# Decoder kernel on one core: softplus to PSUM, its product with u on VectorE, the step copied by ScalarE, and the convolution split around the last sum over states

## What is computed

```python
u, z = jnp.split(layer_norm(x) @ in_w, 2, axis=-1)            # 256 channels each
up = jnp.pad(u, ((0, 0), (3, 0), (0, 0)))
u = silu(cb + sum(up[:, k:k + L, :] * cw[:, k] for k in range(4)))
dbl = u @ xw
dt = softplus(dbl[..., :64] @ dtw + dtb)                      # the step
Bm, Cm = dbl[..., 64:80], dbl[..., 80:]
dA = exp(dt[..., None] * A)                                   # 16 states per channel
dBu = (dt * u)[..., None] * Bm[:, :, None, :]
h = dA_t * h + dBu_t                                          # over time
y = einsum('ben,bn->be', h, C_t)                              # sum over states
x = x + ((y + u * Dp) * silu(z)) @ ow
```

## Time and profile before

| | us |
|---|---|
| median of 3 runs | 1981.62 (1978.43 to 1983.26) |
| profiled execution | 1982.75 |
| its span | 1980.9 |

### The profile page before, as it was taken

The page is one execution under the profiler, slowest core; times in us unless marked ns, Lnnn a source line. Parts: engine busy times, 40 slices in busy tenths (PEclk is TensorE's granted clock), DMA queues, the critical chain, the costliest instruction groups (busy, mean ns, idle before and its releaser), DMA issues. The chain is left out here.

```text
span 1980.9 us, 23714 instructions
## 1 busy us (share of the span) xinstructions
PE 1417.6 (72%) x6931; PEld 753.8 (38%) x6931; DVE 1440.6 (73%) x2510; ACT 1137.4 (57%) x2515; POOL 1200.4 (61%) x759
## 2 busy tenths in 40 slices
PE   3899899995755556655566565556535899999968
PEld 2777577773311112211112121111101566666523
DVE  3666488885508988989898888999984566666734
ACT  2543688884636555555555555555533677777720
POOL 2000356560029999999999999999993243444400
PEclk8999899996567767777677776777866899999978
DMA  3000000000034323343322432333213000000000
GB/s 101 1 1 1 1 2 1 0 1 1 0 132 175 120 111 150 126 153 150 139 97 108 172 150 106 150 150 135 95 70 86 1 1 1 1 0 1 1 0 22
DMA packets 51970, 134.40 MB, mean 68 GB/s; under 512 B 19076, under 2 KB 28568, under 8 KB 39448
## 3 DMA queue, kind: packets, MB, share of 16 engines
q1 hardware_dynamic: 49112, 130.78, 17.4%
q10 hardware_dynamic: 2496, 2.36, 0.4%
q0 software_dynamic: 256, 0.01, 0.0%
HBM read 114.26 MB, written 18.87 MB: 67 GB/s over the span
## 5 line engine op out<-in xcount | busy, mean ns | idle before, releaser
L1470 POOL TENSOR_TENSOR ma_hs<-ma_dtuR,ma_Bt 128x1024 f32<-128x1024 f32 x256 | 596.4, 2353 | 7.1 <-DMA ma_dtuR<-ma_dtu_d 6.9
L1629 ACT ACTIVATE ps<-ma_dtR,ma_A 128x512 f32<-128x512 f32 x512 | 332.7, 682 | 361.2 <-DVE ma_hs L1763 221.3
L786 POOL TENSOR_TENSOR x_pr<-x_pr,x_rec 128x512 f32<-128x512 f32 x256 | 267.5, 1045 | 352.7 <-DVE x_rec L1035 352.7
L1547 PE MATMUL ps<-ma_hs,ma_fold 128*32 128x512 f32 x1024 | 198.4, 915 | 293.8 <-POOL ma_hs L1478 237.3
L1757 DVE TENSOR_TENSOR_SCAN ps<-ps,ma_hs 128x1024 f32<-128x1024 f32 x144 | 329.1, 2286 | 5.7 <-POOL ma_hs L1470 4.5
L1757 DVE TENSOR_TENSOR_SCAN ma_hs<-ps,ma_hs 128x1024 f32<-128x1024 f32 x112 | 255.9, 2284 | 47.1 <-POOL ma_hs L1470 38.6
L1001 ACT ACTIVATE x_pr<-x_sm,x_mx 128x256 f32<-128x256 f32 x512 | 254.5, 500 | 52.5 <-DVE x_mx L1026 52.0
L1478 POOL TENSOR_TENSOR ma_hs<-ma_hs,ma_Ct 128x1024 f32<-128x1024 f32 x112 | 262.9, 2348 | 0.4 <-DVE ma_hs L1757 0.4
L1547 PEld LDWEIGHTS ps<-ma_hs,ma_fold 128*32 128x32 f32 x1024 | 37.9, 144 | 422.4 <-issue 337.7
L1514 PE MATMUL ps<-ma_hn,ma_w_tap 128*128 128x512 f32 (+3 forms) x256 | 147.4, 741 | 59.7 <-ACT ma_hn L1647 47.8
L1763 DVE TENSOR_TENSOR ma_hs<-ps,ma_Ct 128x1024 f32<-128x1024 f32 x144 | 176.3, 1225 | 5.0
(11 more groups left out here) (308 smaller groups left out, 2466.8 us busy)
## 6 DMA issues: line engine op xcount, KB each, us to landing
ma_dtuR<-ma_dtu_d SPq DMA_DIRECT2D x32, 1024.0 KB, 7.0
ma_dtR<-ma_dt_d SPq DMA_DIRECT2D x32, 1024.0 KB, 8.9
ma_Bt<-ma_bc_d SPq DMA_DIRECT2D x16, 1024.0 KB, 5.0
ma_Ct<-ma_bc_d SPq DMA_DIRECT2D x16, 1024.0 KB, 6.9
ma_dtu_d<-ma_dtu SPq DMA_DIRECT2D x32, 256.0 KB, 2.0
ma_dt_d<-ma_dt SPq DMA_DIRECT2D x32, 256.0 KB, 2.3
ma_cwb<-in_L_attn_conv_w_dram SPq DMA_DIRECT2D x4, 512.0 KB
x_m<-in_mask_BxSxS_fk_dram SPq DMA_DIRECT2D x1, 2048.0 KB, 11.2
```

The source lines that it names most:

```text
L786: pool.tensor_tensor(pr[:, r, :, :], pr[:, r, :, :], rec[:, r, :].unsqueeze(2).broadcast_to([P, 2, L]), ALU.mult).then_inc(pr_done, 1)
L1470: pool.tensor_tensor(hs[:, k % SLOTS, :, :], dtuR[:, unit(f, h), q, :].unsqueeze(1).broadcast_to([P, 2, CH]), rows(Bt, k), ALU.mult).then_ ...
L1547: mm = pe.matmul(c.ps[q * E32:(q + 1) * E32, Y[h], :], fold[:, :], hs[:, (k0 + q) % SLOTS, a, :], start=False, stop=(j % 2 == 1 and a == 1 ...
L1629: e = act.activation(c.ps[:, 2 * (k % 2) + a, :], dtR[:, unit(f, h), q, :], ACT.Exp, scale=A[:, (f // QUARTERS) % 2, h, q, no:no + 1])
```

## The change

- VectorE writes softplus back to the PSUM banks PA and PB instead of `dt`, and then multiplies it with u into `dtu`. GpSimd's `dt_times_u` with its products and memsets is gone.
- ScalarE copies the step from PSUM to `dt`, all but the first position of each sequence (`copy_dt`, at t = 9). The large number is set once, at the start of the stage. SP waits for the product before it writes `dtu`, and for the copy before it writes `dt`. TensorE's next use of the banks waits for the copies.
- `NORM_D` is {1, 2, 3, 6, 8, 10, 12, 14, 15}: items 5, 7, 9, 11 and 13 go to GpSimd, and 6, 8, 10, 12 and 14 to VectorE. The two engines keep seven and nine items.
- The taps of channels 0 to 127 come before the last sum, those of 128 to 255 behind it.
- `inv_std`, `affine` (ScalarE) and `scaled_x` (VectorE) come one item earlier.

```diff
-    NORM_D = {1, 2, 3, 5, 7, 9, 11, 13, 15}
+    NORM_D = {1, 2, 3, 6, 8, 10, 12, 14, 15}
...
                         sp.dma_start(dtu_d[d, h], dtu[:, h, :]).then_inc(dt_out[h], 16)
+                        sp.wait_ge(dt_copied, 2 * F + h + 1)
                         sp.dma_start(dt_d[d, h], dt[:, h, :]).then_inc(dt_out[h], 16)
...
+                pool.memset(dt[:, :, :].rearrange("p h (b l) -> p (h b) l", l=L)[:, :, 0:1], BIG).then_inc(consts, 1)
...
-                def dt_times_u(F):
-                    for h in range(2):
-                        pool.wait_ge(dt_done, 2 * F + h + 1)
-                        pool.tensor_tensor(dtu[:, h, :], dt[:, h, :], u[:, F % 2, h, :], ALU.mult).then_inc(first_set, 1)
-                        pool.wait_ge(first_set, 2 * F + h + 1)
-                        pool.memset(by_seq(dt[:, h, :])[:, :, 0:1], BIG).then_inc(dtu_done, 1)
...
-                        if t == 8 and f + 1 < NF:
-                            dt_times_u(f + 1)
...
+                tap_projection(0, 0)
                 for f in range(-1, NF + 1):
                     F, G = f + 1, f + 2
-                    if F < NF:
-                        tap_projection(F)
                     if f >= 1:
                         sum_y(f - 1, 3)
+                    if F < NF:
+                        tap_projection(F, 1)
...
-                        pe.wait_ge(dt_done, 2 * F + 2)
+                        pe.wait_ge(dt_copied, 2 * F + 2)
...
                     if 0 <= f < NF:
                         sum_y(f, 2)
+                    if G < NF:
+                        tap_projection(G, 0)
...
+                def copy_dt(F):
+                    if F >= 1:
+                        act.wait_ge(dt_out0, 32 * F)
+                        act.wait_ge(dt_out1, 32 * F)
+                    for h, bank in ((0, PA), (1, PB)):
+                        act.wait_ge(dtu_done, 2 * F + h + 1)
+                        act.activation(by_seq(dt[:, h, :])[:, :, 1:L], by_seq(c.ps[:, bank, :])[:, :, 1:L], ACT.Copy
+                                       ).then_inc(dt_copied, 1)
...
-                        dve.scalar_tensor_tensor(out=dt[:, h, :], in0=c.ps[:, bank, :], scalar=0.0, in1=dtu[:, h, :],
+                        dve.scalar_tensor_tensor(out=c.ps[:, bank, :], in0=c.ps[:, bank, :], scalar=0.0, in1=dtu[:, h, :],
                                                  op0=ALU.max, op1=ALU.add).then_inc(dt_done, 1)
+                    for h, bank in ((0, PA), (1, PB)):
+                        dve.wait_ge(dt_done, 2 * F + h + 1)
+                        dve.tensor_tensor(dtu[:, h, :], c.ps[:, bank, :], u[:, F % 2, h, :], ALU.mult).then_inc(dtu_done, 1)
```

More of the change, by code:

```diff
@@ L1329, in mamba_stage @@
         names = ("weights_in consts tap_w dd_done a_exp a_done centred squared var_done lnv_done rstd_done scaled "
-                 "hn_done u_ps u_done z_ps z_done x_ps xp_done dt_ps abs_done exp_done ln_done dt_done dtu_done first_set "
+                 "hn_done u_ps u_done z_ps z_done x_ps xp_done dt_ps abs_done exp_done ln_done dt_done dtu_done dt_copied "
                  "bc_out bt_in ct_in dt_out0 dt_out1 dt_in0 dt_in1 dtu_in0 dtu_in1 da_done dbu_done scan_done "
@@ L1333, in mamba_stage @@
         (weights_in, consts, tap_w, dd_done, a_exp, a_done, centred, squared, var_done, lnv_done, rstd_done, scaled,
-         hn_done, u_ps, u_done, z_ps, z_done, x_ps, xp_done, dt_ps, abs_done, exp_done, ln_done, dt_done, dtu_done, first_set,
+         hn_done, u_ps, u_done, z_ps, z_done, x_ps, xp_done, dt_ps, abs_done, exp_done, ln_done, dt_done, dtu_done, dt_copied,
          bc_out, bt_in, ct_in, dt_out0, dt_out1, dt_in0, dt_in1, dtu_in0, dtu_in1, da_done, dbu_done, scan_done,
@@ L1438, in _ @@
                 pool.wait_ge(consts, 3)
+                pool.memset(dt[:, :, :].rearrange("p h (b l) -> p (h b) l", l=L)[:, :, 0:1], BIG).then_inc(consts, 1)
+                pool.wait_ge(consts, 4)
                 pool.affine_select(out=fold[:, :], in_=fold[:, :], compare_op=ALU.is_ge, fill=0.0,
                                    base=0, pattern=[[-NI, E32]], channel_multiplier=1).then_inc(consts, 1)
-                pool.wait_ge(consts, 4)
+                pool.wait_ge(consts, 5)
                 pool.affine_select(out=fold[:, :], in_=fold[:, :], compare_op=ALU.is_ge, fill=0.0,
@@ L1499, in _, with tap_projection @@
                             times_c(k)
-                        if t == 8 and f + 1 < NF:
-                            dt_times_u(f + 1)
             @block.tensor
             def _(pe):
-                def tap_projection(F):
+                def tap_projection(F, h):
                     b = (F // QUARTERS) % 2
[L1507 to L1516, removed]
+                    if h == 0:
+                        pe.wait_ge(tap_w, 3 * (F // QUARTERS) + 3)
+                        pe.wait_ge(hn_done, F + 1)
+                    for e in range(TAPS):
+                        out, src = c.ps[:, (PA, PB)[h], :], hn[:, :]
+                        if e:
+                            out, src = by_seq(out)[:, :, e:L], by_seq(src)[:, :, 0:L - e]
+                        mm = pe.matmul(out, w_tap[:, b, TAPS - 1 - e, h * P:(h + 1) * P], src,
+                                       start=(e == 0), stop=(e == TAPS - 1), skip_group_check=True)
+                    mm.then_inc(u_ps, 1)
                 def gate_projection(F, h, bank):
@@ L1568, in _ @@
                 average(0)
-                pe.wait_ge(consts, 5)
+                pe.wait_ge(consts, 6)
+                tap_projection(0, 0)
                 for f in range(-1, NF + 1):
                     F, G = f + 1, f + 2
-                    if F < NF:
-                        tap_projection(F)
                     if f >= 1:
                         sum_y(f - 1, 3)
+                    if F < NF:
+                        tap_projection(F, 1)
                     if 0 <= f < NF:
@@ L1696, in _ @@
                 logarithm(0)
+                act.wait_ge(consts, 6)
+                copy_dt(0)
                 square(1)
@@ L1717, in _ @@
                                 logarithm(F)
+                            if t == 9:
+                                copy_dt(F)
                         if G < NF:
@@ L1720, in _ @@
                                 square(G)
-                            if t == 13:
+                            if t == 12:
                                 inv_std(G)
-                            if t == 15:
+                            if t == 14:
                                 affine(G)
@@ L1787, in _ @@
                             residual(f - 1)
-                        if t == 14 and G < NF:
+                        if t == 13 and G < NF:
                             scaled_x(G)
```

4 lines of the change are left out of this document (removed).

## The result

The changed kernel takes 1994.62 us (median of 6 runs, 1991.77 to 1995.37) against 1981.14 for the kernel before on the same chip (6 runs): a ratio of 1.0063, 95% interval 1.0049 to 1.0077, so 0.6% slower. Its profiled execution took 1995.02 us.

A forecast was written before the change was run, and what follows sets the result against it. GpSimd's single saturated queue was taken to bound the recurrence. -41.4 + 47.9 + 3.3 = +9.8 us on 1982.75 gave 1992.6, and 1991.5 us for the median, 1.1 lower; range 1968 to 2004.

The forecast's parts named there:

- The gain of 41.4 us: GpSimd's queue in the recurrence: fifteen pairs of step products with their memsets leave, 2.76 us each, 41.4 us less.
- The cost of 47.9 us: GpSimd's B products of items 12 and 16 wait for the second and third sums, 31 times: 47.9 us more.
- The rule s - 2.04: Each GpSimd wait for a second or third sum lasts s - 2.04 us, s being the sum's length.
- The end, 3.3 us: Last quarter: VectorE, held by the gate behind the second sum, ends late, so the last sum ends 3.3 us later.
- The sum, +9.8 us: Whole kernel: -41.4 + 47.9 + 3.3 = +9.8 us against the profiled execution of 1982.75 us.
- the outside: Outside the recurrence no instruction changes, so no time was put down there.
- Prologue and ScalarE's copies at nothing: Prologue's VectorE work replaces similar GpSimd time, and ScalarE's two copies of about 0.60 us are covered: nothing added.
- Rival 2: Second and third sums: the slot wait costs nothing, by full-clock sums or earlier C products; 1943.5 us, chance 0.08.
- Rival 1: Only the second sum bites; the third runs at full clock or starts earlier, 23 us less: 1968, chance 0.09.
- Rival 3: The chain from gate 1 over silus and decay 4 delays item 4's scan: about 2003 us, chance 0.12.
- The split convolution: Last sum of a quarter starts after half the taps, shortening only VectorE's wait before gate 1, which was free.

The follow-up runs named there:

- the ninth slot: The changed kernel with nine slots of hs instead of eight, a B product waiting for the sum one product later: 1946.23 us, ratio 0.9833.
- the third sum alone: The changed kernel with VectorE's C products at {1, 2, 3, 5, 7, 10, 12, 14, 15}, so only the third sum's C product stays moved: 1964.09 us, ratio 0.9919.
- the added matmuls: The changed kernel with sixteen extra matmuls behind the dt projection and three on each side of the average matmul: 1947.87 us, ratio 0.9831.
- the first experiment: The changed kernel with VectorE's C products back at the old items {1, 2, 3, 5, 7, 9, 11, 13, 15}: 1938.93 us, repeated on another chip 1938.2 us.
- the sixteen matmuls: The changed kernel with sixteen extra matmuls behind the dt projection, ahead of the second sum only: 1970.23 us, ratio 0.9943.
- the two whole ones: Two runs of the changed kernel with the old items and the whole convolution ahead of the last sum: 1943.08 and 1941.55 us.
- ten items: The changed kernel with the old items, and item 10's C product also on VectorE in every second quarter: 1923.4 us, ratio 0.9718.

## Why the prediction was right

The forecast was 1991.5 us, the result 1994.62; against the kernel before, +9.8 us were forecast and +13.5 measured (1981.14 to 1994.62). The mechanism is the one forecast, and the terms can be held against the profile one by one.

- **The gain of 41.4 us.** The profile shows 40.9 us less busy time of GpSimd over the whole span; that counts the pair ahead of the recurrence too, and the B and C products took 3.0 us more in all (862.3 us instead of 859.3), so that between the first B product and the last C product it is 38.3 less (867.4 instead of 905.7). In time, with the items put back, the kernel is 41 us faster than before (1938.2 against 1979.09), where 41.4 had been forecast: the step part was worth its place in the queue.
- **The cost of 47.9 us.** Measured 31 waits and 47.3 us. The rule s - 2.04 gives 1.60 for a sum of 3.64 us and 1.38 for one of 3.42; the rows show 1.58 and 1.44. The handoff from TensorE to GpSimd, put at 0.08, was 0.10. That these waits go into the time one for one, and that they hang on the slot and on the length of the sum, is shown by the ninth slot, the third sum alone and the added matmuls.
- **The end, 3.3 us.** The last C product on GpSimd ends at 1505.97, the last sum at 1512.94: 6.97 us, where it was 3.78, so 3.2.
- **The sum, +9.8 us.** From the first instruction of the stage to the end of the last sum it was 957.70 us (546.72 to 1504.42) and is 967.73 (545.21 to 1512.94): +10.0.
- **What the sum left out.** The profiled executions differ by 12.3 us. The stages ahead ran 1.5 us shorter and those behind 3.8 longer, though nothing changed there; 1.6 of these are the norm's first matmuls, 5.24 us in place of 3.67. I had set the outside at nothing. The 3.8 us are within what differs from run to run: the kernel of the first experiment takes 480.2 us behind the stage in one profile and 474.2 in the other, where these two kernels take 476.5 and 480.3. So how well the total was met beyond the stage is luck.
- **Prologue and ScalarE's copies at nothing.** Between the stage's first instruction and GpSimd's first B product lie the same 45.6 us as before. Two waits for a copy show, and neither reaches GpSimd: TensorE waits once, 6.1 us, in the prologue, and SP 15 times for at most 0.4 us, 5.4 in all, before it sends the step.
- **Rival 2** was the one that the rule of the Trainium skill led to ("TensorE: Matmul & The Clock Gate", "What's actually happening": for the slow start, under 1% of a typical kernel's span). The trace does not agree for this kernel: the waits for 31 sums, which ran at half clock for most of their length or all of it, are 47.3 us, 2.4% of the span, because a full queue stands behind them. The added matmuls then brought just this rival about: 1947.87 us, where it had been put at 1943.5.
- **Rival 1**, a short third sum, did not come; its price (23 us) is what the sixteen matmuls measured for the second sum (24.4). **Rival 3** did not come either, but its margin is thin: with the ninth slot the scan of item 4 is what GpSimd waits for next. (With ten items it is that of item 12, behind the added product, in three quarters, 0.4 to 0.5 us each, and that of item 14 in the last, 1.5.)
- **The split convolution** was said to shorten only a free wait; the two whole ones bear that out. The three steps of the norm that come one item earlier were not tried alone; with the items back, GpSimd's queue has no pause left that they could shorten or cause.
- What I didn't see: the way through PSUM looked like a detail that costs a copy. It is what makes the move to VectorE pay: without it the kernel takes 2037.68 us, 59 more than before the change.

What stays open: where the last 3.7 us between the forecast and the measured difference of the medians lie (the stage of one profiled execution of each kernel shows 0.2 of them), and why VectorE's product stood behind GpSimd in twelve quarters and not in three.

## What to carry to other kernels

Work that leaves a saturated queue takes its cover with it: list the waits of that queue whose slack was this work, and place the last producer of each batch so that the consumer that frees a buffer has time to finish; where that can't be, one more buffer does it. A short burst on TensorE that a full queue waits for is priced at the length that it shows in the trace, after its pause, not at that of the full clock. And before a product goes to VectorE beside a busy GpSimd, see that one of its inputs is in PSUM.

## What the runs showed of the hardware

- VectorE's product of 128x512 with both inputs in SBUF took up to 11.2 us instead of 0.68 while GpSimd ran products back to back. In 12 of 15 pairs the first product ended only once GpSimd had paused; in three it ended after one product of GpSimd. GpSimd's own products took 2.37 us on average, and 2.80 in the six places where VectorE came in between.
- A pause of 4.91 us after 10.47 us of matmuls at a stretch (at a granted clock of 1.00) left the next sum at 0.50, that is 1.2 GHz, and 3.64 us; behind pauses of 1.24 and 1.49 us sums ran at 1.00, 2.4 GHz, and 1.92 us. What ran before counts too: with sixteen added matmuls a second sum 2.73 us behind 13.90 us of matmuls took 1.92 us, and third sums 2.81 us behind an average matmul of 2.07 us took 3.64.
